# Twelve more gathers of odd sizes behind the last one, and a few register-addressed copies and loads in layer 1

## The reference, cut to what matters

```python
# layer 0: u is one row, since batch is all zero
m   = relu(concat([x[dst], x[src], edge_attr, u], 1) @ W1.T + b1)      # 200000 x 128
agg = segment_sum(m, dst, 6250)
x   = layernorm(x + relu(concat([x, agg, u], 1) @ W2.T + b2))

# layer 1
h   = relu(concat([x[src], x[dst], edge_attr], -1) @ msg_w1 + msg_b1)
m   = h @ msg_w2 + msg_b2
agg = segment_sum(m, dst) / max(count(dst), 1)                         # zero where count is 0
x   = layernorm(x + relu(concat([x, agg], -1) @ upd_w1 + upd_b1) @ upd_w2 + upd_b2)
```

## Time and profile before

| | |
|---|---|
| median of 3 runs | 3929.05 us (3928.67 to 3929.61) |
| profiled execution, span from first to last instruction | 3929.8 us |
| POOL busy | 2960.2 us (75%) |
| PE busy | 3229.0 us (82%), weight loads 2975.7 us (76%) |
| DVE busy | 1583.8 us (40%) |
| ACT busy | 590.4 us (15%) |
| mean granted TensorE clock | 0.560 |
| HBM traffic over the span | 142 GB/s |

### The profile page before, as it was taken

The page is one execution under the profiler, slowest core; times in us unless marked ns, Lnnn a source line. Parts: engine busy times, 40 slices in busy tenths (PEclk is TensorE's granted clock), DMA queues, the critical chain, the costliest instruction groups (busy, mean ns, idle before and its releaser), DMA issues.

```text
span 3929.8 us, 45222 instructions
## 1 busy us (share of the span) xinstructions
PE 3229.0 (82%) x16881; PEld 2975.7 (76%) x16881; DVE 1583.8 (40%) x3640; ACT 590.4 (15%) x1017; POOL 2960.2 (75%) x3156
## 2 busy tenths in 40 slices
PE   6988888888788888888878888878888888888887
PEld 6877777777777777777778777777777777777776
DVE  6533334343444444444543333333433333333333
ACT  1211111111111111111111111111111111111111
POOL 7777777777777777777777777777777777777776
PEclk7755555565655556665665555555555555555556
DMA  7644444444444444445454444444444444444443
GB/s 261 200 138 134 135 136 143 132 133 139 148 139 149 149 149 147 147 147 154 131 158 135 133 131 124 135 139 136 139 136 141 139 142 137 140 135 141 142 142 100
DMA packets 257760, 563.18 MB, mean 143 GB/s; under 512 B 131254, under 2 KB 151713, under 8 KB 232572
## 3 DMA queue, kind: packets, MB, share of 16 engines
q1 hardware_dynamic: 132824, 332.20, 25.4%
q0 software_dynamic: 100032, 205.00, 19.8%
q10 hardware_dynamic: 24676, 23.01, 1.7%
HBM read 537.29 MB, written 22.66 MB: 142 GB/s over the span
## 4 chain that ended last, share of the span: by engine, by line
POOL 70%; issue 23%; DMA 4%; DVE 2%; PE 2%; ACT 0%; SPq 0%; POOLq 0%; DVEq 0%
POOL Qr L319 70%; DMA Qr<-tabQ,srcE 3%; DVE BIG L1405 1%; PE bank L1137 0%; DMA srcE<-in_srcL 0%; DVE BIG L1302 0%; PE bank L1119 0%; PE bank L1092 0%; DVE BIG L1392 0%; DMA tabQ<-BIG 0%; DVE BIG L1400 0%; PE bank L1051 0%; PE bank L1045 0%; DVE AC L609 0%; POOL Qr L325 0%
## 5 line engine op out<-in xcount | busy, mean ns | idle before, releaser
L319 POOL DMA_INDIRECT Qr<-tabQ,srcE x3094 | 2925.3, 945 | 942.9 <-issue 933.2
L1137 PE MATMUL bank<-BIG 128*128 128x42 f32 x6252 | 1379.0, 396 | 143.6 <-ACT BIG L1287 141.1
L1119 PE MATMUL bank<-wall,BIG 128*128 128x128 f32 x6252 | 1473.0, 410 | 19.1 <-DMA BIG<-tabP 19.1
L1137 PEld LDWEIGHTS bank<-BIG 128*128 128x128 f32 x6252 | 1307.5, 308 | 207.6 <-ACT BIG L1287 201.5
L1302 DVE TENSOR_TENSOR BIG<-bank,BIG 126x512 bf16<-126x512 f32 x782 | 539.3, 690 | 2264.7 <-DMA Qr<-tabQ,srcE 2254.8
L1119 PEld LDWEIGHTS bank<-wall,BIG 128*128 128x128 f32 x6252 | 1311.5, 309 | 23.8 <-issue 23.8
L1287 ACT ACTIVATE BIG<-BIG 128x512 f32<-128x512 f32 (+1 forms) x782 | 492.1, 629 | 3229.1 <-DVE BIG L1405 3220.4
L1124 PE MATMUL bank<-BIG 126*128 126x128 bf16 x3126 | 490.2, 295 | 506.5 <-DVE BIG L1302 396.7
L1124 PEld LDWEIGHTS bank<-BIG 126*128 126x128 bf16 x3126 | 342.0, 135 | 639.0 <-DVE BIG L1302 455.9
L1405 DVE TENSOR_TENSOR BIG<-bank,Qr 128x512 f32<-128x512 f32 (+1 forms) x782 | 532.7, 681 | 41.2 <-PE bank L1124 25.3
L1392 DVE TENSOR_TENSOR BIG<-bank,relE 128x168 f32<-128x168 f32 x782 | 252.6, 323 | 3.5 <-DMA Qr<-tabQ,srcE 3.5
(11 more groups left out here) (137 smaller groups left out, 609.9 us busy)
## 6 DMA issues: line engine op xcount, KB each, us to landing
BIG<-in_eaT SPq DMA_DIRECT2D x194, 1024.0 KB, 5.4
BIG<-in_dstR SPq DMA_DIRECT2D x194, 504.0 KB
Qr<-tabQ,srcE POOLq DMA_INDIRECT x3094
BIG<-tabP SPq DMA_DIRECT2D x526, 31.5 KB
tabP<-BIG ACTq DMA_DIRECT2D x22, 384.0 KB, 3.1
tabQ<-BIG ACTq DMA_DIRECT2D x17, 256.0 KB, 5.2
X<-in_xN SPq DMA_DIRECT2D x1, 3136.0 KB, 16.8
tabE<-BIG ACTq DMA_DIRECT2D x11, 256.0 KB, 2.3
```

Of the source, the lines that this page charges most:

```text
L319: e.indirect_dma_start(Q[0:p, i % R_Q, j, :], None, table[:, :], bass.IndirectOffsetOnAxis(ap=srcE[0:p, g, j:j + 1], axis=0)).then_inc(f_q ...
L1119: e.matmul(bank[i % R_C][:, j * D:(j + 1) * D], f_eaT[:, k % R_EA, (g % LQ * J + j) * P:(g % LQ * J + j + 1) * P], wc[l], start=(j == 0), ...
L1137: last = e.matmul(sums[:, 0:W], M[:, i % R_M, j, :], S[:, hot(i), j, :], start=(j == 0 and first_of(i)), stop=(j == n - 1 and last_of(i)))
```

## The change

On GpSimd, behind the last gather of layer 1, twelve more gathers from the same table: eleven with 128, 127, 127, 126, 126, 120, 112, 96, 64, 16 and 128 rows of 512 bytes, and one with 128 half rows of 256 bytes, seen as a table with two entries a row. They write into dstE and count up a semaphore of their own, on which GpSimd then waits until all twelve have landed. In layer 1 ScalarE copies sixteen single columns of XT, at positions from registers, ahead of group 100's relu; VectorE does the same in group 110, and then loads its window registers anew; the sync engine loads sixteen single rows of tabQ in group 120, ahead of that group's window load, and waits for them at the very end. All of these write into srcB. Nothing reads what the new instructions write.

```diff
+SHAPES = (128, 127, 127, 126, 126, 120, 112, 96, 64, 16, 128)
+COLUMNS = 16
...
+        s_shape, s_line = gs[1]["g"], gs[1]["all"]
...
+        cols = srcB[:, :].bitcast(F32)
...
+                    if i == NG + 120:
+                        _, lines = nc.values_load_multi_w_load_instructions(
+                            baseI[0:1, 0:COLUMNS], engines=[mybir.EngineType.SP], min_val=0, max_val=N - 1,
+                            skip_runtime_bounds_check_because="the first destination of a group, which is a node")
+                        for c in range(COLUMNS):
+                            e.dma_start(cols[c:c + 1, 2 * COLUMNS:2 * COLUMNS + D], tabQ[1][bass.ds(lines[c], 1), :]).then_inc(s_line, 16)
...
+            e.wait_ge(s_line, 16 * COLUMNS)
             for h in range(2):
                 e.wait_ge(u_o[h], 16 * len(range(h, NU, 2)))
...
             gathers(e, 1, EARLY, NG, tabQ[1])
+            spare = dstE[:, :, :].rearrange("p g j -> p (g j)").bitcast(F32)
+            for k, p in enumerate(SHAPES):
+                e.indirect_dma_start(spare[0:p, k * D:(k + 1) * D], None, tabQ[1][:, :],
+                                     bass.IndirectOffsetOnAxis(ap=srcE[0:p, k, 0:1], axis=0)).then_inc(s_shape, 16)
+            k = len(SHAPES)
+            e.indirect_dma_start(spare[:, k * D:k * D + D // 2], None, tabQ[1].rearrange("n (h d) -> (n h) d", h=2),
+                                 bass.IndirectOffsetOnAxis(ap=srcE[:, k, 0:1], axis=0)).then_inc(s_shape, 16)
+            e.wait_ge(s_shape, 16 * (len(SHAPES) + 1))
...
+                    if l == 1 and g == 100:
+                        _, at = nc.values_load_multi_w_load_instructions(
+                            baseI[0:1, 0:COLUMNS], engines=[mybir.EngineType.Activation], min_val=0, max_val=N - 1,
+                            skip_runtime_bounds_check_because="the first destination of a group, which is a node")
+                        for c in range(COLUMNS):
+                            e.copy(cols[:, c:c + 1], XT[:, bass.ds(at[c], 1)])
...
+                    if l == 1 and g == 110:
+                        _, at = nc.values_load_multi_w_load_instructions(
+                            baseI[0:1, 0:COLUMNS], engines=[mybir.EngineType.DVE], min_val=0, max_val=N - 1,
+                            skip_runtime_bounds_check_because="the first destination of a group, which is a node")
+                        for c in range(COLUMNS):
+                            e.tensor_copy(cols[:, COLUMNS + c:COLUMNS + c + 1], XT[:, bass.ds(at[c], 1)])
+                        loaded = None
```

## The result

The changed kernel takes 3939.45 us (median of 7 runs, 3938.51 to 3940.56) against 3929.05 us for the kernel before (7 runs, 3928.23 to 3930.54). The ratio is 1.0027, with a 95% interval of 1.0015 to 1.0038: 10.4 us slower, 0.26%. The profiled execution has a span of 3938.8 us, 9.0 more than the one of before.

What follows compares the result with a forecast made beforehand. GpSimd's gathers were taken as the bound, about 3,865 of 3,929.8 us. Twelve gathers, landing, branch and drain past its hidden exit end the span at 3935.6: +5.8 on 3929.05 gives 3934.9 us, range 3931.5 to 3940.3.

Steps and rivals of the forecast that it cites:

- the place of the loss: GpSimd's exit: twelve gathers, landing, branch and drain reach past the other engines' end, adding 5.8 us of span.
- the hidden parts: Groups 100 to 120: copies and loads on ScalarE, VectorE and the sync queue, covered by the ring of ten groups; nothing.
- No change: Whole kernel: outcome within about 0.2% of the time before, given chance 0.64.
- mark of 0.2%: Whole kernel: about what a measurement can tell from no change, 7.9 us.
- the 3 us put down: Groups 100 and 110: sixteen narrow copies take 3.2 us on ScalarE, at most 3.0 on VectorE, hidden.
- Rival E: Layer 1: VectorE's narrow copies hold up GpSimd's gathers, 2.7 us above forecast, 3937.6 us, +0.22%; chance 0.02.
- I take the straight line, since its two ends are 5% apart: Twelve added gathers: time from 0.85 us fixed plus 0.7 ns a row, read off 64 and 128 rows.
- Rival C: Twelve added gathers: odd shapes cost GpSimd more, up to 6 us, +11.8 us, 3940.9 us; chance 0.06.
- the one-engine rule: Gathers of 127 rows: all rows go to one DMA engine, 3.9 us instead of 0.25, landing before the twelfth.
- I see no reason why that should stand still meanwhile: GpSimd's drain: the 7.2 us after the last gather run on during wait and branch, so it ends at 3935.4.
- rival B: GpSimd's drain: 7.2 us of work starting when it arrives; span +10.4 us, time 3939.4, 0.26% slower; chance 0.27.
- The row of 0.19 us: GpSimd's drain ahead of any gather: took 0.19 us, read as showing a drain with nothing outstanding is short.

Runs made afterwards that it cites:

- f3: Kernel before plus one gather of 127 rows behind the last one and a wait for its landing; one run 3935.45 us against 3932.99.
- e6_wait_last_norm: Kernel before plus only a wait for ScalarE's last normalisation ahead of GpSimd's branch; 3935.7 us against 3929.07, ratio 1.0016.
- f1: Changed kernel without GpSimd's wait for the twelve gathers; 3938.59 us against 3932.99 for the kernel before, ratio 1.0015.
- e1: Changed kernel with only the twelve gathers and GpSimd's wait, no column copies or row loads; ratio 1.0011, on the 4765.33 us chip.
- e7: Changed kernel with row counts 128, 125, 121, 119, 117, 113, 97, 95, 61, 31, 128; no kernel time given, listed gathers 0.96 to 2.35 us.
- g1: Kernel before plus twelve gathers, the first of 127 rows and eleven of 128, and the wait; one run 3949.88 us against 3930.1.
- f2: Changed kernel with 128 rows in all eleven whole-row gathers; 3944.4 us against 3932.99 for the kernel before, ratio 1.0031.
- e5: Kernel before plus only a wait for the landing of GpSimd's last gather ahead of its branch; one run 3930.39 us against 3929.07.

## Why the prediction was right and wrong

The range (3931.5 to 3940.3) held 3939.45, and the bound of the kernel, the place of the loss and the hidden parts were as said. The forecast of 3934.9 was 4.6 us too low. "No change" as the likeliest outcome was wrong by the prediction's own mark of 0.2%, though that mark lies inside the measured interval (0.15 to 0.38%).

**What held.** Copies, loads and the sync queue cost nothing. The sixteen copies took 1.6 to 1.7 us, less than the 3 us put down. Rival E (copies that hold up gathers) shows nothing in the trace. ScalarE's drain stood at 3928.3 and GpSimd's exit alone set the end. The wait moved the branch behind the gathers, with the 2.7 us to the drain exposed.

**First step that failed: "I take the straight line, since its two ends are 5% apart".** The line ran through 64 and 128 rows, which have quotients of 4 and 8. In the terms that the time follows, the two were neighbours, and 127 rows lay far outside. Measured, the two gathers cost 1.62 us more each; the other ten followed the line within 0.06 us. Term: 14.8 us forecast, 18.3 measured. Rival C had this size (up to 6 us) at 0.06. The prediction did weigh the one-engine rule, but only for the data's way through the DMA engine. Its 31 ns a row were about right (29 in f3) and stayed hidden here, since the last landing came 1.5 us after the last gather. The cost was GpSimd's own 13.3 ns a row, serial with everything behind it.

**Second step that failed: "I see no reason why that should stand still meanwhile".** The drain's 7.2 us do stand still: they are work that starts when the drain arrives and all gathers before it are done. e6_wait_last_norm shows it without a single gather more, and it is rival B's mechanism. The row of 0.19 us was read as the drain's own cost with the rest a wait; it was the cost with no gather behind it.

**Why B's number came out, and the range held.** B gave 3939.4 us and the result is 3939.45. That is luck, by two errors that cancel: the drain after the change is 3.98 us and not 7.25 (3.3 less), and the gathers took 3.5 us more than B had. The range held by the same luck: with the gathers as measured and the 7.25 us of e6 as the drain, the time would have been some 3.3 us longer, about 3942.7 (an estimate from these two rows), beyond its upper end. The sum from measured terms is 3912.17 + 18.26 + 1.49 + 2.67 + 3.98 + 0.24 = 3938.8, the span. Against the kernel before, GpSimd's last gather ends 16.97 us later, and from there to the end of its drain are 8.14 us instead of 7.19. Of these 17.9 us, 8.95 were free, since its drain used to end that much ahead of the release (3920.65 to 3929.6). That leaves the 9.0 of the spans. From the last gather to the end of the span are 8.4 us with the wait and 4.2 without (f1).

**What stays open.** Why the drain is 3.98 us after the change, in e1, e7 and after the no-wait form (3.92), with row counts that differ, and 8.2 with twelve full gathers or one gather of 127 rows among full ones. Several uneven gathers seem to be needed; which of them, and what they settle ahead of the drain, no run told. A rival to that was not tested: a mark in the number of elements for each engine, empty ones counted. The gathers behind the last old one add 322 of them after the change and in e1 and 407 in e7, where the drain is short, but only 215 in g1, 127 in f3 and 96 in f2, where it is long. g1's theory 1 counted rows alone and put the change at about 195, so g1 does not exclude a mark between 215 and 322.

## What to carry to other kernels

An engine that is done early is not free to be given work or a wait, since its exit is hidden only where it ends before the others are done. A sequencer that runs ahead hides the landing (here 1.5 us) and the way from branch to drain (2.7); the drain's own 4 to 8 us come behind the last gather in either case (f1). One wait ahead of the exit cost 6.6 us with no work behind it (e6). A cost read off two sizes holds for sizes of the same kind; for gathers on GpSimd choose a row count with a divisor near 16, since 127 rows cost 2.56 us and 128 cost 0.94. Before a chance is put on a cause that is "somewhere in the wait", look which terms start on arrival, since those add to whatever comes late.

## What the runs showed of the hardware

A gather on GpSimd takes 0.86 us and 13.3 ns for each row of the count divided by its largest divisor up to 16, within 0.02 us over the 22 whole-row gathers of the changed kernel and of e7. The packets of e7 show that engines without rows get empty elements of 4 bytes in the same number. A gather of 127 rows moved its rows one packet after another at 29 ns a row and needed 7.5 us from start to landing (f3), against 2.8 for 128 rows.

GpSimd's drain is 0.19 us before any gather and 7.25 us after 3,126 (e5, e6), from its arrival on or, where it stands in the queue already, from the end of the last gather. It was 0.08 us longer for each of up to twelve gathers more, but 3.98 us with the uneven ones of the changed kernel and of e7. It was the same to 1 ns on two chips (3.975 and 3.976, 8.232 twice). The same program took 3929 us on one chip, 3933 on another and 4765 on a third, where GpSimd waited for VectorE's sums; why, the experiments did not ask.
